# Two tiles per transfer, scratch rows laid out by step, and eleven extra matmuls of weights at the start

## The reference, cut to what matters

```python
e = stack([tbl_f[ids[:, f]] for f in range(32)], axis=1)      # (1024, 32, 16)
xk = x0 = e
for W in (W0, W1, W2):                                        # (32, h, 64), h = 32, 64, 64
    xk = relu(einsum('bmd,bhd,mhk->bkd', x0, xk, W))
    outs.append(sum(xk, axis=2))
z = concatenate(outs, axis=1)                                 # (1024, 192)
h = concatenate([z, dense_ctx], axis=1)
h = maximum(h @ W_top1 + b_top1, 0)
h = maximum(h @ W_top2 + b_top2, 0)
y = h @ W_top3
```

## Time and profile before

| what | value |
|---|---|
| median of 3 runs | 625.69 us (624.11 to 625.83) |
| the profiled execution: time, span | 622.48 us, 620.7 us |
| busy: PE, DVE, POOL, ACT | 563.6 (91%), 546.5 (88%), 488.3 (79%), 308.2 us (50%) |
| DMA: moved, mean rate | 150.89 MB, 243 GB/s |
| transfers x0bc<-x_rows | 256 of 512 KB, 7.0 us median from issue to landing |
| transfers x0g<-x_rows | 16 of 512 KB, 4.7 us |

### The profile page before, as it was taken

The page is one execution under the profiler, slowest core; times in us unless marked ns, Lnnn a source line. Parts: engine busy times, 40 slices in busy tenths (PEclk is TensorE's granted clock), DMA queues, the critical chain, the costliest instruction groups (busy, mean ns, idle before and its releaser), DMA issues.

```text
span 620.7 us, 7817 instructions
## 1 busy us (share of the span) xinstructions
PE 563.6 (91%) x2548; PEld 194.8 (31%) x2548; DVE 546.5 (88%) x321; ACT 308.2 (50%) x1345; POOL 488.3 (79%) x364
## 2 busy tenths in 40 slices
PE   0058997999999999999999999999999999999997
PEld 0012232332322333333333333333333333334354
DVE  0038997999999999999999999999999999999580
ACT  0023735355464745455476736454565736454442
POOL 6765888887889798988888788988888797949360
PEclk9997999999999999999999999999999999999998
DMA  3198878778586868788686858787776858687000
GB/s 99 29 375 315 309 249 310 274 267 295 191 314 210 316 218 311 270 299 295 223 289 215 310 199 313 261 310 274 251 275 213 289 212 311 255 306 271 2 1 0
DMA packets 52852, 150.89 MB, mean 243 GB/s; under 512 B 9830, under 2 KB 17386, under 8 KB 52810
## 3 DMA queue, kind: packets, MB, share of 16 engines
q1 hardware_dynamic: 44608, 148.27, 65.6%
q0 software_dynamic: 8192, 2.11, 2.5%
q10 hardware_dynamic: 10, 0.00, 0.0%
HBM read 147.20 MB, written 3.15 MB: 242 GB/s over the span
## 4 chain that ended last, share of the span: by engine, by line
DVE 33%; PE 29%; DMA 19%; issue 8%; POOL 8%; SPq 2%; ACT 1%; DVEq 0%; POOLq 0%
DVE prod L336 31%; PE y_ps L518 26%; DMA x0bc<-x_rows 14%; POOL emb L291 6%; DMA emb<-table,row_sb 2%; DVE z L364 2%; DMA x_rows<-emb 2%; PE x0g_ps L579 2%; POOL pool_prod L306 2%; SPq L263 1%; PE x0g_ps L584 1%; PE x0g_ps L602 0%; SPq L236 0%; SPq L246 0%; DMA off_sb<-id_offset 0%
## 5 line engine op out<-in xcount | busy, mean ns | idle before, releaser
L336 DVE TENSOR_TENSOR prod<-x0bc,x_ps 128x2048 f32<-128x2048 f32 (+1 forms) x252 | 456.5, 1887 | 13.6 <-ACT x_ps L418 13.1
L518 PE MATMUL y_ps<-prod,w_sb 128*64 128x512 f32 x1640 | 381.2, 598 | 12.2 <-DVE prod L336 12.0
L291 POOL DMA_INDIRECT emb<-table,row_sb x256 | 244.9, 957 | 65.5 <-issue 62.8
L306 POOL TENSOR_TENSOR pool_prod<-x0bc,x_sb 128x1024 f32<-128x1024 f32 x102 | 242.4, 2384 | 48.1 <-ACT x_sb L435 35.0
L518 PEld LDWEIGHTS y_ps<-prod,w_sb 128*64 128x64 f32 x1640 | 115.5, 137 | 253.4 <-issue 214.0
L425 ACT ACTIVATE relu<-y_ps 128x16 f32<-128x16 f32 x480 | 79.6, 296 | 115.3 <-PE y_ps L518 115.3
L418 ACT ACTIVATE x_ps<-y_ps 64x512 f32<-64x512 f32 x128 | 73.0, 570 | 75.4 <-PE y_ps L518 72.8
L518 PE MATMUL y_ps<-pool_prod,w_sb 128*64 128x512 f32 x408 | 104.9, 594 | 2.1 <-POOL pool_prod L306 2.0
L336 DVE TENSOR_TENSOR prod<-x0bc,x0g_ps 128x2048 f32<-128x2048 f32 x32 | 72.8, 2288 | 37.5 <-DMA x0bc<-x_rows 32.4
L435 ACT ACTIVATE x_sb<-relu 64x512 f32<-64x512 f32 x128 | 80.4, 628 | 3.4
L425 ACT ACTIVATION_READ_ACCUMULATOR relu<-y_ps 128x1 f32 x480 | 79.7, 322 | 0.0
(11 more groups left out here) (34 smaller groups left out, 71.0 us busy)
## 6 DMA issues: line engine op xcount, KB each, us to landing
x0bc<-x_rows SPq DMA_DIRECT2D x256, 512.0 KB, 7.0
x0g<-x_rows SPq DMA_DIRECT2D x16, 512.0 KB, 4.7
emb<-table,row_sb POOLq DMA_INDIRECT x256
x_rows<-emb SPq DMA_DIRECT2D x16, 128.0 KB, 2.1
w_sb<-w SPq DMA_DIRECT2D x2, 512.0 KB, 4.7
x_rows<-emb SPq DMA_DIRECT2D x16, 64.0 KB, 2.0
wt_sb<-wt SPq DMA_DIRECT2D x1, 512.0 KB
wt1a_sb<-wt_a SPq DMA_DIRECT2D x1, 256.0 KB
```

The costliest lines, as they stand in the source:

```text
L291: pool.indirect_dma_start(emb[:, turn, DIM * n:DIM * (n + 1)], None, table, bass.IndirectOffsetOnAxis(row_sb[:, at:at + 1], 0)).then_inc(g ...
L306: pool.tensor_tensor(pool_prod[:, n % POOL_RING, 0:width(s)], x0bc[:, slot(s, j), 0:width(s)], x[:, 0:width(s)], ALU.mult).then_inc(pool_p ...
L336: made = dve.tensor_tensor(out, left, right, ALU.mult)
L518: made = pe.matmul(ps[MAPS * h:MAPS * (h + 1), 0:half(s)], w, moving[:, half(s) * h:half(s) * (h + 1)], start=first, stop=final)
```

## The change

- The scratch tensor becomes flat, and a step's 48 rows lie one behind the other (`rows_at(s)`, row pitch 4 KB where it was 64 KB). Rows f and f + 1 of a step are then contiguous.
- A transfer brings two tiles (`MOVED = 2`): SHIFT of an even tile and the next one differ by 1, so each partition gets one run of 8 KB. There are eight transfers of 1 MB for a step instead of sixteen of 512 KB. The waits of the two tiles for their slots are joined, and the semaphores `bc_in` are split by the step's parity.
- The order on SP is written anew: `store_rows(s + 1)` and `load_x0g(s + 1)` are issued at the end of `load_tiles(s)`. With `AHEAD` empty, that is the same place as before with respect to stores, x0g and tiles.
- The seven MLP loads, all issued behind the tiles of step 1 and ahead of `store_rows(2)` before, are now spread: `wt1a` after `load_tiles(1)`, `wt1b`, `wt3`, `bt1`, `bt2` after `load_tiles(2)`, `wt2` and the dense features after `load_tiles(3)`. As `load_tiles(s)` ends with x0g of step s + 1, they stand between that x0g and the first tiles of step s + 1.
- PE, which waited for its first work, now waits for the store of step 0 and then runs eight matmuls of w1 with 512 columns of w2 (`keep_going((0, 0), 8)`), whose result is overwritten, and three more after the first layer 0.
- `GATHERED_FIRST = 2` and `copies_after` leave gathers and waits what they were.

```diff
+MOVED = 2
-def slot(s, j):
-    return (TILES * s + j) % SLOTS
+def tile_columns(s, j, count=1):
+
+    lead = j - j % MOVED
+    at = PAIR * ((TILES * s + lead) % SLOTS) + width(s) * (j - lead)
+    return slice(at, at + width(s) * count)
+
+
+def rows_at(s):
+
+    return X0_ROWS * DIM * FIRST_ROW[s]
...
-        x0bc = sb("x0bc", [P, SLOTS, PAIR])
+        x0bc = sb("x0bc", [P, SLOTS * PAIR])
...
-        bc_in = [sem(f"bc_in{g}") for g in range(TILES // GROUP)]
+        bc_in = [[sem(f"bc_in{i}_{g}") for g in range(TILES // MOVED)] for i in range(2)]
...
                 for a, b in ((0, FIELDS), (FIELDS, X0_ROWS)):
-                    sp.dma_start(x0_rows[a:b, cols].rearrange("f (q c) -> f q c", q=QUART),
-                                 emb[0:QUART * (b - a), turn, 0:DIM * GATHERS_OF[s]]).then_inc(scratch_out[turn], 16)
+                    rows = bass.AP(x0_rows.tensor, rows_at(s) + a * width(s), [[c, QUART * (b - a)], [1, c]])
+                    sp.dma_start(rows, emb[0:QUART * (b - a), turn, 0:c]).then_inc(scratch_out[turn], 16)
...
             def load_x0g(s):
+                sp.wait_ge(scratch_out[s % 2], 32 * (s // 2 + 1))
...
-                rows = bass.AP(x0_rows.tensor, DIM * FIRST_ROW[s],
-                               [[COLS, FIELDS], [QUART * COLS, QUART], [1, width(s)]])
+                rows = bass.AP(x0_rows.tensor, rows_at(s),
+                               [[width(s), FIELDS], [QUART * width(s), QUART], [1, width(s)]])
...
             def load_tiles(s):
-                for j in range(TILES):
+                store_at, load_at = AHEAD.get(s, (TILES, TILES))
+                for j in range(0, TILES + MOVED, MOVED):
+                    if s + 1 < STEPS:
+                        if j == store_at:
+                            store_rows(s + 1)
+                        if j == load_at:
+                            load_x0g(s + 1)
+                    if j == TILES:
+                        break
                     k = TILES * s + j
                     if k >= SLOTS:
-                        wait_free(k - SLOTS)
-                    rows = x0_rows[SHIFT[j]:SHIFT[j] + FIELDS, columns(s)].unsqueeze(1).to_broadcast(
-                        [FIELDS, QUART, width(s)])
-                    sp.dma_start(x0bc[:, slot(s, j), 0:width(s)], rows).then_inc(bc_in[j // GROUP], 16)
+                        wait_free(*divmod(k - SLOTS, TILES))
+                    rows = bass.AP(x0_rows.tensor, rows_at(s) + SHIFT[j] * width(s),
+                                   [[width(s), FIELDS], [0, QUART], [1, MOVED * width(s)]])
+                    sp.dma_start(x0bc[:, tile_columns(s, j, MOVED)], rows).then_inc(bc_in[s % 2][j // MOVED], 16)
...
+            store_rows(0)
+            load_x0g(0)
             for s in range(STEPS):
-                store_rows(s)
-                sp.wait_ge(scratch_out[s % 2], 32 * (s // 2 + 1))
-                load_x0g(s)
                 load_tiles(s)
-                if s == 1:
-                    for dst, src in ((wt1a_sb[:], wt1_a), (wt1b_sb[:], wt1_b), (wt2_sb[:], wt2), (wt3_sb[:], wt3),
-                                     (bt1_sb[:], bt1), (bt2_sb[:], bt2), (zt_b[MAPS:, :], dense_t)):
-                        sp.dma_start(dst, src).then_inc(mlp_in, 16)
+
+                for dst, src in {1: ((wt1a_sb[:], wt1_a),),
+                                 2: ((wt1b_sb[:], wt1_b), (wt3_sb[:], wt3), (bt1_sb[:], bt1), (bt2_sb[:], bt2)),
+                                 3: ((wt2_sb[:], wt2), (zt_b[MAPS:, :], dense_t))}.get(s, ()):
+                    sp.dma_start(dst, src).then_inc(mlp_in, 16)
...
+            def keep_going(x, count):
+
+                for _ in range(count):
+                    pe.matmul(y_bank(x)[0:MAPS, :], w1_sb[:, 0, :], w2_sb[:, 0:HALF // MAPS, :], start=True, stop=True)
...
             pe.wait_ge(w0_ready, 2)
+
+            pe.wait_ge(scratch_out[0], 32)
+            keep_going((0, 0), 8)
             layer0(0)
+            keep_going((0, 1), 3)
...
-    x0_rows = nc.dram_tensor("x0_rows", [X0_ROWS, COLS], F32, kind="Internal").ap()
+    x0_rows = nc.dram_tensor("x0_rows", [X0_ROWS * COLS], F32, kind="Internal").ap()
```

More of the change, by code:

```diff
@@ L51 @@
 GATHERS_AFTER = {1: [1, 1, 8], 2: [1, 1, 4]}
-def columns(s):
-    return slice(DIM * FIRST_ROW[s], DIM * FIRST_ROW[s + 1])
+GATHERED_FIRST = 2
+AHEAD = {}
 def width(s):
@@ L140, in summed2_after, with copies_after @@
     return FIRST_ROW[min(s + 1, LAST)] // 2 + (1 if s == LAST else 0)
-def slot(s, j):
-    return (TILES * s + j) % SLOTS
+def copies_after(s, l):
+    return 4 * sum(1 for i in range(s + 1) if pool_tiles(i, l + 1))
+def tile_columns(s, j, count=1):
[4 more added lines that the diff above has]
+    return X0_ROWS * DIM * FIRST_ROW[s]
 def cin_tower_kernel(nc, table, ids, id_offset, dense_t, w0_a, w0_b, w0_sq, w1, w2,
@@ L256, in load_tiles, with wait_free @@
-            def load_tiles(s):
-                for j in range(TILES):
+            def wait_free(s, j):
+                own = range(j, j + MOVED)
+                by_pool = [t for t in own if t in pool_tiles(s, 2)]
+                by_vector = [t for t in own if t not in by_pool]
+                if by_pool:
+                    sp.wait_ge(pool_products, pool_before((s, 2)) + pool_tiles(s, 2).index(by_pool[-1]) + 1)
+                if by_vector:
+                    sp.wait_ge(products, before((s, 2)) + by_vector[-1] // GROUP + 1)
@@ L299, in layer @@
                 done = 0 if l == 1 else sum(GATHERS_AFTER[1])
-                pool.wait_ge(copied[l - 1], 4 * (s + 1))
+                pool.wait_ge(copied[l - 1], copies_after(s, l - 1))
                 for k, j in enumerate(pool_tiles(s, l)):
-                    pool.wait_ge(bc_in[j // GROUP], 32 * (s + 1))
+                    pool.wait_ge(bc_in[s % 2][j // MOVED], 16 * (s // 2 + 1))
                     n = pool_before((s, l)) + k
@@ L305, in layer @@
                         pool.wait_ge(pool_products_used, n - POOL_RING + 1)
-                    pool.tensor_tensor(pool_prod[:, n % POOL_RING, 0:width(s)], x0bc[:, slot(s, j), 0:width(s)],
+                    pool.tensor_tensor(pool_prod[:, n % POOL_RING, 0:width(s)], x0bc[:, tile_columns(s, j)],
                                        x[:, 0:width(s)], ALU.mult).then_inc(pool_products, 1)
-                    if s + 2 < STEPS:
+                    if GATHERED_FIRST <= s + 2 < STEPS:
                         gather(s + 2, done, done + gathers[k])
@@ L318, in _ @@
             pool.wait_ge(rows_done, 2)
-            gather(1, 0, GATHERS_OF[1])
+            for s in range(1, GATHERED_FIRST):
+                gather(s, 0, GATHERS_OF[s])
             pool.wait_ge(w0_ready, 2)
@@ L330, in product @@
                     dve.wait_ge(products_used, n - RING + 1)
-                at, count = slot(s, group[0]), len(group)
+                count = len(group)
                 halves = slice(0, 2) if h is None else slice(h, h + 1)
+                tiles = x0bc[:, tile_columns(s, group[0], count)].rearrange("p (t c) -> p t c", t=count)
                 out, left = (t.rearrange("p t (h c) -> p t h c", h=2)[:, :, halves, :]
-                             for t in (prod[:, n % RING, 0:count, 0:width(s)], x0bc[:, at:at + count, 0:width(s)]))
+                             for t in (prod[:, n % RING, 0:count, 0:width(s)], tiles))
                 right = x[:, halves, 0:half(s)].unsqueeze(1).to_broadcast(list(left.shape))
@@ L342, in layer0 @@
                 for g, group in enumerate(groups_of(s, 0)):
-                    dve.wait_ge(bc_in[g], 32 * (s + 1))
+                    dve.wait_ge(bc_in[s % 2][group[0] // MOVED], 16 * (s // 2 + 1))
                     product(s, before((s, 0)) + g, group, x0g_ps)
@@ L430, in finish @@
                 act.activation(relu[:, l, 0:half(s)], ps[:, 0:half(s)], ACT.Relu).then_inc(relu_done[l], 1)
-                if x is not None:
+                if x is not None and pool_tiles(s, l + 1):
                     act.wait_ge(relu_done[l], s + 1)
```

2 lines of the change are left out of this document (1 added, 1 removed).

## The result

Seventeen runs of each kernel: 623.23 us median after (618.62 to 625.84), 625.69 before (623.35 to 628.75). The ratio is 0.9964, 95% interval 0.9948 to 0.9981: faster by 0.2 to 0.5%, some 2.3 us. The forecast was 624.5, with a range of 620.8 to 627.5. The direction was right, but the prediction gave "faster" a chance of 0.36 and "within 0.3%" one of 0.51, and 623.23 lies at the lower edge (623.2) of the forecast's own range, nearer to the 622.7 of its first rival. The profiled execution took 621.02 us (span 619.2) where that of before took 622.48: 1.5 us less, where the sum gave 1.2.

What follows compares the result with a forecast made beforehand. DVE was taken to bound up to step 4, then PE, leaving at most 1.9 us until 541 and nothing after. Terms of -0.35 and -0.9 us gave about -1.2, so 625.7 became 624.5 us, range 620.8 to 627.5.

Steps and rivals of the forecast that it cites:

- MLP loads: Moving them lands step 2's gathers 1.5 us sooner; their new places cost 0.65 us at step 2, 1.2 and 1.5 later.
- first rival: The new layout makes each step's first pair land 0.6 us earlier, not 0.2: centre 622, chance 0.27.
- the sum: Gains of 0.35 us up to step 4 and 0.9 us from steps 5 to 15, together about -1.2 us.
- The chain of the gates: Last gather, store to HBM, x0g, first pair of tiles; a gate is the landing of a step's first pair.
- the signs that would have made the prediction wrong: No wait at steps 3 and 4, x0g and pair shorter by over half a microsecond, or GpSimd starting after 53.
- gate of step 2: First pair's landing: GpSimd -0.6, gathers -1.5, wt1a +0.65, transfer -0.2; -1.7 us in all, to 99.0.
- the rival of the other side: The late gathers of step 2 aren't the MLP loads' doing: 626.8 us, or 627.5; chance 0.16.
- The extra matmuls: At PE's start: first layer 1 products about 1.2 us earlier, GpSimd's start unmoved, cost and gain 0 to 0.3 us.
- Two tiles per transfer: Tile loads gain 0.2 us a gate (bounds 0 and 0.4) and 0.6 us on step 0's 8.5 MB.
- The brake of "at most 1.9 us": From step 5 on at most 1.9 us can be gained, PE's total wait for DVE from 201 to 541 us.
- The rule on row pitch: Copy rates are lower at large power-of-two pitches; taken as absent here, otherwise it counts with the rival centred on 622.
- The carry-over to the median: The runs' median lies 3.2 us above the profiled execution; added unchanged, it turns 621.3 into 624.5 us.

Runs made afterwards that it cites:

- the run with the old place: The changed kernel with all seven MLP loads back between the tiles of step 1 and the store of step 2: 0.9941, 622.79 us.

## Why the prediction was right or wrong

**The chain of the gates: right as a chain, its close figures partly luck.** The gates were forecast at 62.0, 99.0 and 133.8, then a lead of 0.3 to 0.4 us at step 4. DVE's products came at 62.07, 99.42, 134.07 (no wait) and with a lead of 0.3. Of the signs that would have made the prediction wrong none appeared: step 4 waits, x0g and the first pair together are 0.3 us shorter, GpSimd starts at 52.29.

Term by term the gate of step 2 was not right. GpSimd's last gather ended 0.2 us sooner (forecast 0.6), the gathers landed 2.2 sooner (1.5), store to x0g took 0.3 less (not in the sum), and from x0g to the product it took 1.4 us more (0.45 forecast). The errors cancel. The way from x0g to the product at step 2 lies between 6.8 and 9.7 us in the kernels with pairs, and it is 9.7 in one that has no MLP load behind x0g at all, so it isn't wt1a's price alone; its cause is open. Against the profiled execution the sum of -1.2 us met -1.5; the second profiles of the two kernels are 4.5 us apart (626.85 and 622.39, taken on two chips), so that agreement is luck too.

**MLP loads: right, gain and price both larger.** The gathers land 2.2 us sooner, not 1.5; moving the loads alone, to the start, is worth 0.3% (0.9969), and the rival of the other side, that they weren't the cause, is refuted by this. The price at step 4 was forecast at 1.5 less slack: the wait is 1.21 us, 1.14 to 1.16 in three further kernels or runs, and gone with the loads at the start. From x0g to the landing of the first pair at step 4 it takes 8.8 to 9.3 us with the loads between (four profiles with pairs) and 6.2 to 7.3 without (three), so they cost 1.5 to 3.2 us there. By the time of the run with the old place, gain and price cancel; its profile doesn't show how.

**The extra matmuls: right for this change, with a wait overlooked.** "Cost and gain: 0 to 0.3 us" holds on the changed kernel within what the runs can tell (0.9937 without, 0.9964 and 0.9952 with; 0.9927 and 0.9929 with the loads at the start). On the kernel before they cost 0.6%. The prediction said that GpSimd's start doesn't move, and did not go on to ask what PE, now earlier, would wait for next and what its clock does then. The fall behind this wait moves GpSimd's second layer by 0.7 us, or by 1.6 to 2.0. That is a price the sum left out, but it doesn't explain the 3 to 3.6 us on the kernel before, and the fall isn't the extra matmuls' alone: the kernel before with the MLP loads at the start has it without them, and is faster than before. What costs the rest is open.

**Two tiles per transfer: the term that was too small.** I took 0.2 us a gate, the middle of 0 and the 0.4 us between the median and the fastest landing of x0g. The comparison of one tile and two with all else kept gives 0.4 to 0.5% (1.0004 against 0.9964 and 0.9952), 3 us or so. Two other pairs of kernels agree: 0.9986 for the rows alone against 0.9941 with pairs and extra matmuls, the loads in the old place in both, and 0.9969 against 0.9927 for rows and pairs together, with intervals that just overlap. So the pairs carry the gain.

What the traces show of it is in line but smaller: from x0g to the second pair's landing, mean over steps 5 to 15, 10.7 us in both kernels with one tile and the new rows, 9.7 to 10.4 in seven profiles with pairs (mean 10.0), 10.2 to 10.6 in four with the rows and tiles of before (mean 10.4). So 0.6 us a gate against the one-tile transfer, 0.35 against before. GpSimd starts at 51.3 to 52.5 in the six profiles with pairs and at most eight extra matmuls ahead of layer 0, at 52.5 to 53.4 in the four of before: 1 us sooner on average, not 0.6. In the one-tile kernel the late tile 13 and a fall of the clock bring GpSimd's layer 2 2.9 us later than in the changed kernel, and with it the gate of step 2 (102.42 for 99.42); steps 2 to 4 have DVE waits of 6.3 us at layer 0, for 3.6. The brake of "at most 1.9 us" behind step 5 was read from one profile; it is 3.6 in the second. How the gain splits between the fewer transfers and the longer runs isn't settled, since two tiles in one transfer need contiguous rows here.

**The rule on row pitch.** The rows alone give 0.9986 (0.9966 to 1.0005). x0g lands 0.9 us sooner, which the earlier trace rows spoke against. The Trainium skill (DMA: Bandwidth & Descriptors, Latency and other measured facts) gives rates that fall as the row pitch of copies between HBM tensors grows from 512 KB to 4 MB. The gain on x0g has the same sign, but at 64 KB and on a load into SBUF, for which that section has no figure. The first pair behind x0g does not come sooner. Whether pitch is the mechanism was not tried.

**The carry-over to the median.** The sum was made on an execution of 622.48 us, and "I carry the difference over" assumed that the change leaves alone the 3.2 us by which the median lies above it. The second profile of the kernel before has 13.9 us of waits for tiles instead of 10.1. A change that shortens this chain may have more to gain in such executions: -1.5 us between the first profiles, -4.5 between the second ones, -2.5 between the medians. That the waits are the reason is argued from two profiles, not shown.

## What to carry to other kernels

When a start is made faster, follow the engine to its next wait and read the clock there: here a lead that the next gate absorbed was worth nothing, and behind the wait that it made the clock fell in front of a backlog. Small loads between the first and the last transfer of a gate cost at least their size (1.5 to 3.2 us here for 0.59 MB, forecast 1.5); where nothing was gated they cost nothing that could be measured. When a sum meets the measurement, compare it term by term: here errors of up to 1 us cancelled. Where a profile of one execution lies at the edge of the runs, take a second one before adding up terms of a microsecond.

## What the runs showed of the hardware

- The clock rose to its upper level while PE ran matmuls that all write the same half of the outputs: in the changed kernel sixteen of them from 27.96 on, and the next full group runs eight MATMULs in 1.94 us, where the kernel before took 3.7.
- The clock went from 2.4 to 1.2 GHz at or behind PE's wait for GpSimd in seven profiles (waits of 2.75 us in the kernel before with the MLP loads at the start, 3.25, 3.50, 3.55, 3.63, 3.79 and 3.88 us in those with extra matmuls) and did not in one (3.39 us). PE's wait for x ahead of that is 3.72 us in six profiles without extra matmuls: the group behind it ran eight MATMULs in 1.94 us in one of them, and in the others the clock fell in this wait or soon behind it. The wait's length alone does not decide it.
- Such a fall moved GpSimd's second layer by 0.7 us in five profiles and by 1.6 and 2.0 us in the two where it lasted longer.
- The last gather of step 2 was followed by its store after 2.8 to 4.6 us where 1 MB of loads had been issued just ahead (five profiles) and after 1.3 to 1.7 us where they had not (nine).
- The same kernel's transfers vary from one execution to the next: x0g's issue to the second pair's landing is 10.2 us on average in one execution of the kernel before and 10.6 in another.
